# Second attention's context: one norm in place of two, values ahead of the keys over four PSUM banks, keys turned two batches later

## What is computed

```python
def _layernorm(x, eps=1e-05):
    return (x - mean(x)) / sqrt(var(x) + eps)

x = x + tanh(g_xattn[1]) * _L1_xattn_ref(_layernorm(x), ctx_1024, ...)

def _L1_xattn_ref(x, context, ...):
    xn = layer_norm(x, ln_in_g, ln_in_b)          # a second norm on the first; eps 1e-5
    cn = layer_norm(context, ln_ctx_g, ln_ctx_b)
    q = xn @ Wq
    k, v = split(cn @ Wkv)                        # 16 heads of 64
    k, v = concat(k, null_k), concat(v, null_v)   # 77 + 1 keys
    q = l2_normalize(q) * q_scale
    k = l2_normalize(k) * k_scale
    attn = softmax(q k * 8)
    return layer_norm((attn v) @ Wo, ...)
```

## Time and profile before

| | us |
|---|---|
| runs of the kernel before | 2010.17, 2000.35, 2000.96 |
| median | 2000.96 |
| span of the profiled execution | 2007.2 |
| PE busy in the span | 1773.6 (88%) |
| DVE, ACT, POOL busy | 1262.0, 975.4, 528.7 |
| mean granted clock of PE | 0.929 of 2.4 GHz |

### The profile page before, as it was taken

The page is one execution under the profiler, slowest core; times in us unless marked ns, Lnnn a source line. Parts: engine busy times, 40 slices in busy tenths (PEclk is TensorE's granted clock), DMA queues, the critical chain, the costliest instruction groups (busy, mean ns, idle before and its releaser), DMA issues. The chain is left out here.

```text
span 2007.2 us, 32563 instructions
## 1 busy us (share of the span) xinstructions
PE 1773.6 (88%) x11808; PEld 1447.6 (72%) x11808; DVE 1262.0 (63%) x2310; ACT 975.4 (49%) x1739; POOL 528.7 (26%) x492
## 2 busy tenths in 40 slices
PE   6998899967799996699999969998899789798895
PEld 4667799922577775699999558886577566688884
DVE  6886488546245553588887566765434688656643
ACT  4652476413687671377776234443433255317730
POOL 2220343254333341222220630002000144213333
PEclk9998799988799996699999979999699899899997
DMA  3003377420100000567775220000000100026742
GB/s 109 17 17 126 121 255 248 132 61 0 49 1 12 6 12 25 203 225 229 246 238 169 81 102 1 1 1 1 22 1 1 57 12 12 30 79 208 235 127 81
DMA packets 97139, 178.32 MB, mean 89 GB/s; under 512 B 25184, under 2 KB 61946, under 8 KB 95914
## 3 DMA queue, kind: packets, MB, share of 16 engines
q1 hardware_dynamic: 85496, 146.00, 22.0%
q0 software_dynamic: 11232, 30.69, 5.2%
q10 hardware_dynamic: 288, 0.00, 0.0%
HBM read 149.38 MB, written 27.26 MB: 88 GB/s over the span
## 5 line engine op out<-in xcount | busy, mean ns | idle before, releaser
L1667 POOL DMA_INDIRECT f_block_rows_home<-normed_x,f_token_of_sb x138 | 168.3, 1220 | 451.4 <-PE psum L1713 324.5
L1693 PE MATMUL psum<-f_block_h_sb,f_w1h_home 128*128 128x256 f32 x736 | 211.4, 287 | 30.2 <-issue 10.7
L1693 PE MATMUL psum<-f_block_l_sb,f_w1h_home 128*128 128x256 f32 x736 | 206.8, 281 | 0.0
L1693 PE MATMUL psum<-f_block_h_sb,f_w1l_home 128*128 128x256 f32 x736 | 206.7, 281 | 0.0
L2316 PE MATMUL psum<-a_xT_home,context_w 128*128 128x256 f32 x704 | 182.2, 405 | 13.6 <-PEq L122 9.7
L1703 PE MATMUL psum<-f_w2h_home,f_hidden_h_home 128*128 128x256 f32 x644 | 187.4, 291 | 2.0 <-DVE f_hidden_l_home L1887 1.0
L1703 PE MATMUL psum<-f_w2h_home,f_hidden_l_home 128*128 128x256 f32 x644 | 181.7, 282 | 0.0
L1703 PE MATMUL psum<-f_w2l_home,f_hidden_h_home 128*128 128x256 f32 x644 | 181.7, 282 | 0.0
L1693 PEld LDWEIGHTS psum<-f_block_h_sb,f_w1h_home 128*128 128x128 f32 x736 | 140.8, 191 | 38.5 <-issue 28.6
L2316 PEld LDWEIGHTS psum<-a_xT_home,context_w 128*128 128x128 f32 x704 | 132.6, 198 | 45.3 <-issue 20.0
L2481 ACT ACTIVATE a_probsT_sb<-psum 77x1024 f32<-77x1024 f32 (+1 forms) x128 | 130.7, 1021 | 69.0 <-PE psum L2368 66.5
(11 more groups left out here) (314 smaller groups left out, 3986.6 us busy)
## 6 DMA issues: line engine op xcount, KB each, us to landing
f_w_sb<-in_f_w SPq DMA_DIRECT2D x161, 512.0 KB
sorted_y<-f_result_sb SPq DMA_DIRECT2D x69, 256.0 KB
normed_x<-f_xn_all SPq DMA_DIRECT2D x24, 256.0 KB, 2.1
f_b_row_sb<-in_f_b SPq DMA_DIRECT2D x46, 128.0 KB
f_w_sb<-in_f_w SPq DMA_DIRECT2D x23, 256.0 KB
f_block_rows_home<-normed_x,f_token_of_sb POOLq DMA_INDIRECT x138
residual<-in_x SPq DMA_DIRECT2D x8, 256.0 KB, 6.2
context_w<-in_a_wk SPq DMA_DIRECT2D x2, 1024.0 KB, 5.0
```

The costliest lines, as they stand in the source:

```text
L1667: nc.gpsimd.indirect_dma_start(block_rows[b % 2][:, h, :], None, xs, bass.IndirectOffsetOnAxis(ap=column, axis=0)).then_inc(sems[f"rows_in ...
L1693: last = nc.tensor.matmul(hid_ps(q)[:, m, :], w, rhs, start=(j == 0), stop=(j == len(parts) - 1))
```

## The change

- **One norm for two.** The first norm leaves a row with variance v / (v + eps); the second divides by the root of that plus eps. Together this is one division by the root of v (1 + eps) + eps squared. `rows_part` makes this variance in one instruction; `normalise_once`, `variance_again` and `normalise_again` go, with their two semaphores and POOL's second inverse root. Rows are normalised in one pass, one batch (two tiles) at a time.
- **Values first.** All 16 value units come ahead of the keys, over banks 0 to 3 in turn. The projections of keys use banks 4 to 7, their turned form banks 0 and 1, the turned rows banks 2 and 3.
- **Keys turned two batches behind.** PE, in round b: projection b, rows of batch b - 2, keys of batch b - 2. ACT: copy and squares of b, rows and keys of b - 2. DVE: sum of b, rows of b, multiply of b - 1. The turn of the first keys also waits for the last value unit's copy.
- **Gathered rows.** `COMBINED` becomes (5, 11) for the first expert layer: five rows by the second closing block and eleven by the third, instead of one and seven.

```diff
-        nc.vector.tensor_scalar(var[:, tiles], mv[:, tiles, 1], EPS, None, ALU.add).then_inc(sems["var_done"], 1)
+        if own:
+            last = nc.vector.tensor_scalar(var[:, tiles], mv[:, tiles, 1], 1.0 + EPS, EPS * EPS, ALU.mult, ALU.add)
+        else:
+            last = nc.vector.tensor_scalar(var[:, tiles], mv[:, tiles, 1], EPS, None, ALU.add)
+        last.then_inc(sems["var_done"], 1)
...
-    V_BANKS = 1 if own else 4
-    VALUES_FIRST = 10
-    v_bank = lambda j: psum[0:CTX, 6 if own else 4 + j % 4, 0:VN]
+    V_BANKS = 4
+    v_bank = lambda j: psum[0:CTX, (0 if own else 4) + j % 4, 0:VN]
     k_bank = lambda j: psum[:, j % 4, 0:HALF]
-    key_banks = lambda b: slice(4 * (b % 2), 4 * (b % 2) + 2)
+    key_banks = lambda b: slice(4 + 2 * (b % 2), 6 + 2 * (b % 2))
...
-            if b == 2:
-                rows["power"](pool, 1, slice(0, TILES))
...
-        return range(2 * b - NBATCH, 2 * b - NBATCH + 2) if b >= NBATCH // 2 else range(0)
+        return range(b - 2, b - 1) if 2 <= b < NBATCH else range(NBATCH - 2, NBATCH) if b == NBATCH else range(0)
...
-        project(0)
-        project(1)
-        project(2)
-        for j in range(VALUES_FIRST):
-            value_products(pe, j)
-        for b in range(NBATCH):
-            if VALUES_FIRST + b < len(v_list):
-                value_products(pe, VALUES_FIRST + b)
-            if b + 3 < NBATCH:
-                project(b + 3)
-            for k in rows_beside(b):
-                rows["turn"](pe, k)
+        def turn_keys(b):
             pe.wait_ge(sems["k_normed"], b + 1)
             if b:
                 pe.wait_ge(sems["kn_out"], b)
+            else:
+                pe.wait_ge(sems["v_out"], len(v_list))
...
+        for j in range(len(v_list)):
+            value_products(pe, j)
+        for b in range(NBATCH + 2):
+            if b < NBATCH:
+                project(b)
+            for k in rows_beside(b):
+                rows["turn"](pe, k)
+            if b >= 2:
+                turn_keys(b - 2)
...
+        for j in range(len(v_list)):
             own_values_out(j)
...
+        for b in range(NBATCH + 2):
+            if b < NBATCH:
+                take(b)
+                squares(b)
             for k in rows_beside(b):
                 rows["turned_out"](act, k)
-            spread(b)
+            if b >= 2:
+                spread(b - 2)
...
+        for b in range(NBATCH + 1):
+            if b < NBATCH:
+                sum_squares(b)
+                rows["normalise"](dve, 0, b)
+            if b:
+                normalise_keys(b - 1)
...
-    COMBINED = (1, 7) if shared == 1 else (4, 12, 20)
+    COMBINED = (5, 11) if shared == 1 else (4, 12, 20)
...
-        return (lambda tile: free[tile // 4][:, tile % 4 * D:(tile % 4 + 1) * D]), (1, None), lambda b: psum[:, 7, :]
+        return (lambda tile: free[tile // 4][:, tile % 4 * D:(tile % 4 + 1) * D]), (2, None), lambda b: psum[:, 2 + b % 2, :]
```

More of the change, by code:

```diff
@@ L258, in rows_part @@
     sems = {k: env["sem"](f"{name}r_{k}") for k in (
-        "loaded", "chain", "var_done", "rstd_done", "once", "stats2", "x_normed", "x_turned", "x_out")}
+        "loaded", "chain", "var_done", "rstd_done", "x_normed", "x_turned", "x_out")}
     ln_in = sb("ln_in", [P, 2, DC]) if own else None
@@ L290, in normalise @@
         last.then_inc(sems["x_normed"], 1)
[L292 to L318, removed]
     def turn(pe, b):
@@ L343, in rows_part @@
     return dict(load=load, load_late=load_late, variance=variance, power=power, normalise=normalise,
-                normalise_once=normalise_once, variance_again=variance_again, normalise_again=normalise_again,
                 turn=turn, turned_out=turned_out)
@@ L588, in own_keys @@
                 pe.wait_ge(sems["kn_out"], b)
+            else:
+                pe.wait_ge(sems["v_out"], len(v_list))
             for c in range(NC):
-                last = nc.tensor.transpose(psum[:, 2 + c // 4, (c % 4) * keys:(c % 4 + 1) * keys],
+                last = nc.tensor.transpose(psum[:, c // 4, (c % 4) * keys:(c % 4 + 1) * keys],
                                            kn[b % 3][:, 2 * c:2 * c + 2, :].rearrange("p h d -> p (h d)"),
@@ L650, in spread @@
                     keysT[:, part * 4:part * 4 + 4, b, :],
-                    psum[:, 2 + part, 0:4 * keys].rearrange("p (c k) -> p c k", k=keys), ACT.Copy, scale=k_scale[:])
+                    psum[:, part, 0:4 * keys].rearrange("p (c k) -> p c k", k=keys), ACT.Copy, scale=k_scale[:])
             last.then_inc(sems["kn_out"], 1)
[L654 to L657, removed]
+        for j in range(len(v_list)):
             own_values_out(j)
[L659 to L667, removed]
+        for b in range(NBATCH + 2):
+            if b < NBATCH:
+                take(b)
+                squares(b)
             for k in rows_beside(b):
                 rows["turned_out"](act, k)
-            spread(b)
+            if b >= 2:
+                spread(b - 2)
     def scalar(act):
@@ L727, in sum_squares, with normalise_keys @@
             nc.vector.tensor_scalar(ss[b % 3][:], ss[b % 3][:], 1e-24, None, ALU.max).then_inc(sems["squared"], 1)
-        sum_squares(0)
-        sum_squares(1)
-        for b in range(NBATCH):
+        def normalise_keys(b):
             dve.wait_ge(sems["inverted"], b + 1)
```

## The result

The changed kernel takes 1974.53 us (median of four runs, 1969.83 to 1983.04) against 2005.57 for the kernel before (a fourth run of 2012.97 stands beside the three of the table), a ratio of 0.9847 with a 95% interval of 0.9809 to 0.9886: 31 us less, with 23 to 38 in the interval. The profiled execution took 1983.04 us with a span of 1981.1. The forecast was 1969 in a range of 1959 to 1983.

What follows compares the result with a forecast made beforehand. No engine is full, so a chain of hand-overs was taken to bound the stretch. The stage ends 40.8 us sooner: 2010.17 - 40.8 = 1969.4, or median 2000.96 - 31.9 = 1969.1; forecast 1969, range 1959 to 1983.

Steps and rivals of the forecast that it cites:

- Steps 2 to 5: Key projections 0 to 2 (10.3 us), first turn and projection 3 (to 452.1), four rounds (to 471.5), tail (10.4, to 481.9).
- step 1: Values: 16 units over four banks at 1.72 us each, PE never waiting: 27.5 us, to 435.6.
- step 4: Key rounds: PE's own work 4.76 us, two-round chain 9.56 or 4.78 a round; 4.85 taken, four rounds to 471.5.
- Cover gone, PE's result bank would come free late by the excess; I take nothing.: Start, before the second closing block: DVE's added rows and statistics, about 3 us, fit its 5.69 us wait for PE.
- So PE never waits: Values over four banks: ACT needs 0.59 us a unit, PE 1.72, so 16 units take 27.5 us.
- the rival of the values held beside the gathers: Value units beside POOL's gathers each pay about 4.4 us: at most 16 us lost, 1985; chance 0.08.
- The end was taken as the last key copy: Stage end: last key copy at 522.74 before, 481.9 after, so 40.8 us sooner.
- I take these to be absent: Two long value-copy waits before the change, 8.88 us together, absent from the two shorter runs: median loses 31.9, not 40.8.
- The rule weighed: Key rounds: DVE's product inside POOL's power isn't held, against the skill's exclusive lock; if held, 1979, chance 0.12.
- The clock rivals: 1.2 GHz in the key rounds: +31 us, 2000, chance 0.05; or from the values on: 2022, chance 0.04.
- the slower side: Low clock from the values on: 16 units take 55 us, keys slow too; 53 us more, 2022; chance 0.04.

## Why the prediction was right, and where its steps failed

- **Steps 2 to 5 came as worked out, and step 1 where no gathers ran.** From the values' first record to the last key copy the working has 73.8 us, and the run without gathers 73.65. In the changed kernel itself the keys part is 45.95 against 46.3: first turn, rounds of 4.81 (forecast 4.85) and tail came as worked out. One reading in step 4 was wrong without harm: "PE's own work" of 4.76 adds busy times that overlap. With nothing to wait for (three batches behind) the rounds come 4.41 us apart, so the chain alone, 9.62 in two rounds, set the pace; that "both ends agree" was chance.
- **"Cover gone, PE's result bank would come free late by the excess; I take nothing."** This step failed by 5.3 us, and its ground with it. DVE was not late: it stood idle for 6.97 us. The closing result's completion was, since the new row schedule lets the gathers run on beside the closing blocks; the plain transfers, and the old schedule in the changed kernel, bring it back to time. About 4.3 of the 5.3 us are the wait, and 1.0 is what the block behind it adds at the low clock.
- **"So PE never waits"** in the values failed by 5.1 us. It is the rival of the values held beside the gathers, in part: I gave it up to 16 us at a chance of 0.08. The evidence that I set against it, key projections at full pace beside the gathers, says little: only the first of the three had to be seen in time (by the third, which writes its banks), and in the changed kernel too the first four value units were on time.
- **The end was taken as the last key copy.** The 8.02 us that POOL takes between its last power and the next block were not in the sum; with the keys ended sooner they became the last wait, 3.2 us more. Start, values and end are 13.6 us together, and with the keys' -0.3 the whole shortfall of 13.3.
- **"I take these to be absent"** from ordinary runs, of the 8.88 us of unexplained waits: not borne out. Whether the two shorter runs had them can't be seen, as these have no trace. But they stand in the other profiled executions in which values in the order of before run beside gathers (9.09 and 4.93 us between copies with the merged norm alone, the first copy at 432.72 with (5, 11)), and without gathers the stage is 11.7 shorter. So 40.8 was the gain to start from, and 13.3 of it went: 27.5, where the text had 40.8 - 8.9 = 31.9. The two errors partly cancel, which is luck, and it is why the forecast gain came so near. The measured 31.0, with 23 to 38 in its interval, doesn't tell 27.5 from 31.9; the stage does. Of the 5.5 us that 1969 is off, 4.6 come from the other side: the median before was 2005.57 with the fourth run, not 2000.96.
- **The rule weighed** did not apply. The product starts 0.49 us into a power and takes 1.21 us (459.53 above). POOL's powers have a mean of 2.99 us, less than the 3.26 of the earlier trace rows:

```profile
L476 POOL TENSOR_TENSOR f_c_rnk<-f_c_ss,half 78x16 f32<-78x16 f32 x8 | 24.0, 2994 | 25.3 <-DVE f_c_ss L693 25.3
...
L699 DVE TENSOR_TENSOR f_xn_all<-f_xn_all,f_c_rnk 78x1024 f32<-78x1024 f32 x6 | 7.3, 1215 | 1.3 <-POOL f_c_rnk L476 1.3
```

  The exclusive lock that the Trainium skill states ("SBUF — State Buffer", section "SBUF: two separate sides") would have held the product for the power; here neither engine waits for the other.
- **The clock rivals** fell: 2.4 GHz through all values and rounds. What the Trainium skill tells of another kernel, a clock that swings while the kernel cycles through PSUM banks ("TensorE: Matmul & The Clock Gate", section "A second HAM failure mode: psum-queue depth-cycling"), did not happen here: 16 units over four banks, even with a stop of 2.88 us, kept the clock. It did fall in the run with keys one batch behind, behind waits of 5 us (0.66 to 0.84 in stretches of 10 us from 450 to 510). The sum of the slower side was off: 27.5 for the units and 31 for the keys make 58.5, not 53, so 2027 instead of 2022. Nothing hung on it.

Of the 27.55 us of the stage, the merged norm gives 10.1 alone in the old order; the rest, 17.4, belongs to order, banks and distance together, net of what the late closing result costs. Taking the distance back to one costs 38.9, going back to one bank 8.7 in one execution. Values first with nothing else was not run, so its share stays open.

## What to carry to other kernels

A gap that no row explains is not noise: look what runs beside it in every instance, try it away, and ask whether the new order still has the same neighbour. An end that is read off the last useful instruction needs the ends of the other engines too, above all one whose wait was just hidden. Where an engine's completions come late in bunches, more banks ahead of the reader can take the bunches out of the path: eight kept PE running through the values in two of three traces here, and in the third it stopped for its last unit alone.

## What the runs showed that was not expected

PE's completions reach ACT and DVE up to 14 us late while POOL's 32 indirect transfers are under way, and on time when SP fetches rows in their place by plain ones. The semaphore updates themselves come late and in bunches, 0.06 us from one to the next. The latest was with (1, 7) in the changed kernel: unit 7 was written by 407.38 + 8 x 1.72 = 421.1 and copied at 435.65. The lateness hits whoever waits then: a closing result (11.1 instead of 6.84 us), value units 1 and 2 of the kernel before, units 4 to 8 after. The closing result repeats: 11.1 to 11.4 us behind the first in all eight traces with (5, 11) and gathers, 6.84 in all four with (1, 7). So does the end: where values came late, the last late bunch is seen 2.3 to 3.8 us after POOL's last gather ends (eleven traces). In between it varies: with one value bank none of the copies was late, and the run with keys one batch behind, whose values are those of the changed kernel, lost nothing (27.70). What decides that stays open.

POOL's wait at the end of a block, from its last power to its next instruction, is 8.02 us in a block with the gathers (8.02 as well with three batches behind, 7.69 behind the added power), and at most 5.08 us without them. Why is open.
